# GpSimd's routing scatters move one step later, one behind each row sum and each normalisation

## The reference, cut to what matters

```python
x = x + _L0_attn_ref(_L0_cond_ref(x, cond_1024, ...), ...)
x = x + _L0_ffn_ref(_L0_cond2_ref(x, cond_1024, ...), ...)

# inside _L0_ffn_ref
attn = jax.nn.softmax(scores, axis=-1)
ao = jnp.einsum('bgqst,bgtd->bgqsd', attn, vb)
h1 = hidden_states + proj
x = ln2.reshape(-1, H)                                   # ln2: layer norm of h1
logits = x @ router_weight
top_p, top_i = jax.lax.top_k(jax.nn.softmax(logits, axis=-1), K)
...
padded_tokens = jnp.zeros((T, H), x.dtype).at[dst].set(x[order // K], mode='drop')
fc1 = jax.nn.gelu(jnp.einsum('ech,ehf->ecf', xt, moe_w1))
fc2 = jnp.einsum('ecf,efh->ech', fc1, moe_w2).reshape(T, H)
moe_out = jnp.zeros((N, H), hidden_states.dtype).at[padded_tid].add(weighted)
return h1 + moe_out.reshape(S, B, H)
```

## Time and profile before

| | us |
|---|---|
| median of 3 runs | 1206.87 (1204.98 to 1224.17) |
| the profiled execution | 1220.39 |
| its span, first to last instruction | 1218.6 |

### The profile page before, as it was taken

How to read it: one execution, slowest core, us unless ns; L and a number is a source line. 1 busy time by engine, 2 the same in 40 slices (tenths; PEclk the granted TensorE clock), 3 DMA queues, 4 the chain that set the end, 5 groups by cost and what they waited for, 6 DMA issues and landing times. The chain is left out here.

```text
span 1218.6 us, 25497 instructions
## 1 busy us (share of the span) xinstructions
PE 1120.3 (92%) x8218; PEld 1022.2 (84%) x8249; DVE 921.7 (76%) x2282; ACT 834.2 (68%) x1927; POOL 585.9 (48%) x564
## 2 busy tenths in 40 slices
PE   7899999999998899999987974989999999999994
PEld 4699999999997688788776863788999999999984
DVE  5677777776775689888888863897778888888872
ACT  2467666667665698888886872666676778778771
POOL 0012122121212244888887776377656546556545
PEclk9899999999998899999998996899999999999997
DMA  9524344353321032444444454378878778887853
GB/s 311 127 91 140 100 142 130 108 164 108 114 71 54 22 100 79 128 137 133 132 132 133 129 178 161 112 184 199 191 178 187 194 185 210 209 195 194 206 140 53
DMA packets 119056, 175.47 MB, mean 144 GB/s; under 512 B 13776, under 2 KB 88944, under 8 KB 118896
## 3 DMA queue, kind: packets, MB, share of 16 engines
q1 hardware_dynamic: 92336, 139.63, 37.7%
q0 software_dynamic: 26592, 34.24, 15.1%
HBM read 107.96 MB, written 67.69 MB: 144 GB/s over the span
## 5 line engine op out<-in xcount | busy, mean ns | idle before, releaser
L1268 POOL DMA_INDIRECT out_rows<-y,row x142 | 238.9, 1683 | 196.6 <-DVE y L1869 75.9
L178 PE MATMUL gh<-w2h,hh 128*128 128x256 f32 x568 | 160.8, 283 | 1.1 <-DVE y L1869 1.1
L180 PE MATMUL gh<-w2h,hl 128*128 128x256 f32 x568 | 160.7, 283 | 0.0
L179 PE MATMUL gh<-w2l,hh 128*128 128x256 f32 x568 | 160.7, 283 | 0.0
L1800 DVE TENSOR_TENSOR hl<-h,hh 128x512 fp32r<-128x512 f32 (+1 forms) x172 | 100.9, 596 | 67.1 <-ACT h L1483 62.1
L1246 POOL DMA_INDIRECT slot_rows<-kept,slot x112 | 117.9, 1053 | 32.8 <-issue 29.5
L1482 ACT ACTIVATE hh<-gw 128x512 fp32r<-128x512 f32 (+1 forms) x86 | 45.7, 531 | 107.6 <-issue 98.0
L178 PEld LDWEIGHTS gh<-w2h,hh 128*128 128x128 f32 x568 | 108.9, 192 | 2.2 <-issue 1.2
L179 PEld LDWEIGHTS gh<-w2l,hh 128*128 128x128 f32 x568 | 108.9, 192 | 1.0
L180 PEld LDWEIGHTS gh<-w2h,hl 128*128 128x128 f32 x568 | 108.9, 192 | 0.0
L819 POOL TENSOR_SCALAR spread<-mv 128x2 f32<-128x2 f32 x32 | 7.1, 221 | 211.6 <-DVE mv L967 211.2
(11 more groups left out here) (322 smaller groups left out, 3955.2 us busy)
## 6 DMA issues: line engine op xcount, KB each, us to landing
w1e<-in_moe_w SPq DMA_DIRECT2D x43, 512.0 KB
w2e<-in_moe_w SPq DMA_DIRECT2D x43, 512.0 KB
x_rows<-x SPq DMA_DIRECT2D x64, 256.0 KB, 2.4
xg<-x_rows SPq DMA_DIRECT2D x64, 256.0 KB
xr<-slot_rows SPq DMA_DIRECT2D x28, 532.0 KB
xT<-in_xT SPq DMA_DIRECT2D x32, 256.0 KB, 2.7
x<-in_x SPq DMA_DIRECT2D x32, 256.0 KB, 3.8
out_rows<-res SPq DMA_DIRECT2D x64, 128.0 KB
```

Source lines behind the costliest of these rows:

```text
L178: nc.tensor.matmul(out, at_a(ah), at_b(bh), start=first, stop=False, skip_group_check=True)
L179: nc.tensor.matmul(out, at_a(ah), at_b(bl), start=False, stop=False, skip_group_check=True)
L180: return nc.tensor.matmul(out, at_a(al), at_b(bh), start=False, stop=last, skip_group_check=True)
L1268: g.indirect_dma_start(out=out, out_offset=bass.IndirectOffsetOnAxis(ap=row[m % NR][:, t:t + 1], axis=0), in_=y[m % 2][:, t, :], in_offset ...
```

## The change

The four scatters of a step are taken out of its end. A generator hands them out one at a time: one after each row sum and one after each normalisation, and they are those of the step before (`scatters(k - 1 if k < I2 else k)`). Step 9 has none, the steps 10 to 31 carry those of the steps 9 to 30; step 31 also issues its own four at its end, and from step 32 on all is as it was. The wait for the blanking of the table moves ahead of step 0's normalisations. Nothing else changes, no operation is added or removed.

```diff
--- before.py
+++ after.py
@@ -1219,26 +1219,8 @@
             g.memset(half[:], -0.5).then_inc(halved, 1)
             pool.wait_ge(halved, 1)
 
-            def step(k, has):
-                if has(k - 2):
-                    after(pool, dve_did["mv"], k - 2, U2 - 1)
-                    g.tensor_scalar(spread[:], mv[:, :, 1], LN_EPS, None, ALU.add).then_inc(pool_did["spread"], 2)
-                    after(pool, pool_did["spread"], k - 2, U2 - 1)
-                    after(pool, act_did["nrm"], k - 3, U2 - 1)
-                    g.tensor_tensor(rstd[:], spread[:], half[:], ALU.pow).then_inc(pool_did["rstd"], 2)
-                    for u in places:
-                        after(pool, dve_did["h1"], k - 2, u)
-                        if k > 2:
-                            pool.wait_ge(stored[u], 16 * (k - 2))
-                        g.tensor_tensor(res[u][:], x12[u][:, 0, :], h1[u][:], ALU.add
-                                        ).then_inc(pool_did["res"], 1)
-                if has(k):
-                    for u in places:
-                        after(pool, dve_did["rden"], k, u)
-                        g.tensor_tensor(pw[k % 2][u][:], pw[k % 2][u][:], den[:, u, :].unsqueeze(2)
-                                        .broadcast_to([P, TG * NKV, S]), ALU.mult).then_inc(pool_did["soft"], 1)
-                if k == 0:
-                    pool.wait_ge(pr.blanked, 16 * (E + 1))
+            def scatters(k):
+
                 for m, pair, j in scattered_at(k):
                     pool.wait_ge(routed, m + 1)
                     after(pool, act_did["nrm"], pair, U2 - 1)
@@ -1247,6 +1229,37 @@
                             out=pr.slots, out_offset=bass.IndirectOffsetOnAxis(ap=pr.slot[:, c, j:j + 1], axis=0),
                             in_=pr.rows[:, j, :], in_offset=None, bounds_check=E * N - 1, oob_is_err=False,
                         ).then_inc(pr.scattered[0 if m <= EARLY_BATCH else 2 if m < LATE_BATCH else 1], 16)
+                        yield
+
+            def step(k, has):
+                if k == 0:
+                    pool.wait_ge(pr.blanked, 16 * (E + 1))
+                scatter = scatters(k - 1 if k < I2 else k)
+                if has(k - 2):
+                    after(pool, dve_did["mv"], k - 2, U2 - 1)
+                    g.tensor_scalar(spread[:], mv[:, :, 1], LN_EPS, None, ALU.add).then_inc(pool_did["spread"], 2)
+                    after(pool, pool_did["spread"], k - 2, U2 - 1)
+                    after(pool, act_did["nrm"], k - 3, U2 - 1)
+                    g.tensor_tensor(rstd[:], spread[:], half[:], ALU.pow).then_inc(pool_did["rstd"], 2)
+                    for u in places:
+                        after(pool, dve_did["h1"], k - 2, u)
+                        if k > 2:
+                            pool.wait_ge(stored[u], 16 * (k - 2))
+                        g.tensor_tensor(res[u][:], x12[u][:, 0, :], h1[u][:], ALU.add
+                                        ).then_inc(pool_did["res"], 1)
+                        if has(k):
+                            next(scatter, None)
+                if has(k):
+                    for u in places:
+                        after(pool, dve_did["rden"], k, u)
+                        g.tensor_tensor(pw[k % 2][u][:], pw[k % 2][u][:], den[:, u, :].unsqueeze(2)
+                                        .broadcast_to([P, TG * NKV, S]), ALU.mult).then_inc(pool_did["soft"], 1)
+                        next(scatter, None)
+                for _ in scatter:
+                    pass
+                if k == I2 - 1:
+                    for _ in scatters(k):
+                        pass
 
             pipeline(pool, step)
             out = d["out"].rearrange("t s n -> (t s) n")
```

More of the change, by code:

```diff
@@ L1220, in _ @@
             pool.wait_ge(halved, 1)
+            def scatters(k):
+                for m, pair, j in scattered_at(k):
+                    pool.wait_ge(routed, m + 1)
+                    after(pool, act_did["nrm"], pair, U2 - 1)
+                    for c in range(K):
+                        g.indirect_dma_start(
+                            out=pr.slots, out_offset=bass.IndirectOffsetOnAxis(ap=pr.slot[:, c, j:j + 1], axis=0),
+                            in_=pr.rows[:, j, :], in_offset=None, bounds_check=E * N - 1, oob_is_err=False,
+                        ).then_inc(pr.scattered[0 if m <= EARLY_BATCH else 2 if m < LATE_BATCH else 1], 16)
+                        yield
             def step(k, has):
+                if k == 0:
+                    pool.wait_ge(pr.blanked, 16 * (E + 1))
+                scatter = scatters(k - 1 if k < I2 else k)
                 if has(k - 2):
@@ L1239, in step @@
                                         .broadcast_to([P, TG * NKV, S]), ALU.mult).then_inc(pool_did["soft"], 1)
-                if k == 0:
-                    pool.wait_ge(pr.blanked, 16 * (E + 1))
-                for m, pair, j in scattered_at(k):
-                    pool.wait_ge(routed, m + 1)
-                    after(pool, act_did["nrm"], pair, U2 - 1)
-                    for c in range(K):
-                        g.indirect_dma_start(
-                            out=pr.slots, out_offset=bass.IndirectOffsetOnAxis(ap=pr.slot[:, c, j:j + 1], axis=0),
-                            in_=pr.rows[:, j, :], in_offset=None, bounds_check=E * N - 1, oob_is_err=False,
-                        ).then_inc(pr.scattered[0 if m <= EARLY_BATCH else 2 if m < LATE_BATCH else 1], 16)
+                        next(scatter, None)
[4 more added lines that the diff above has]
+                        pass
             pipeline(pool, step)
```

## The result

The kernel after takes 1252.99 us (median of 6 runs, 1248.91 to 1254.90), the kernel before, run beside it, 1208.82 (6 runs). The ratio is **1.0352, interval 1.0316 to 1.0389**: slower, by some 43 us (44 between the medians). The forecast of 1225 had the sign and less than half of the size, and the range to 1238 did not hold it.

The account below looks back on a forecast made before the run. GpSimd was taken to bound the kernel before, and the ring through the second normalisation the kernel after. The terms -1.0 + 8.9 + 8.4 - 2.7 + 5.1 gave +18.7 us, so 1225 us, range 1205 to 1238.

Parts of the forecast that it names:

- GpSimd bounds the kernel before; the change costs places, not work: Steps 11 to 25: GpSimd sets the pace at 9.98 us a step; nothing is removed or added, so places are costed.
- The row sums' ring: Row sum, SyncE's load, then `mv`: needs 9.6 us a step after the change and does not bind below that.
- Steps 9 to 11, -1.0: Step 9 loses its scatters, step 10 runs at GpSimd's pace: 18.9 us against 19.9.
- The ring through the second normalisation: Second normalisation, TensorE's queue, VectorE's maximum to `mv`: 21.2 us per two steps, +8.9 us over steps 11 to 25.
- The rule weighed: VectorE's two-port mode could lock out GpSimd and lengthen moved scatters; at its worst the sum would be the third rival's.
- Steps 25 to 29 at no cost: These steps are held by VectorE's table and TensorE's late scores, which the ring of 21.2 us hardly exceeds.
- Step 29's stall, 17.9 us: SyncE's load waits for scatters spread over step 29; step 30 starts 17.9 us after it, before 9.57: +8.4 us.
- Step 31, 14.7 us: Step 31 has eight scatters, so step 32 starts 14.7 us after it, against 9.64: +5.1 us.
- Step 30 to 31, -2.7: TensorE and ScalarE catch up during step 29's stall, so 12.35 us become GpSimd's 9.6.
- GpSimd stays the bound: Rival, chance 0.17: TensorE's order may have slack, so steps take 9.63 us; total 1212 us.
- faster: Rival, chance 0.08: scatter issue hides behind compute, at best a pace of 9.24 us a step; total 1198 us.
- Heavier: Rival, chance 0.22: scatters run at 1.44 us where they now stand; +27 us, total 1234 us.

Follow-up runs that it names:

- e11: The kernel before, with GpSimd's first instruction of a step (spread, variances plus a constant) given to VectorE; ratio 1.0047 to the kernel before.
- e4: The kernel after, with three scatters still ahead of the second normalisation but none between the row sums; ratio 1.0372 to the kernel before.
- e1: The kernel after, with all four scatters at the end of the step, behind both normalisations; ratio 1.0119 to the kernel before.
- e13: The kernel after, with two and four useless matmuls ahead of TensorE's two waits for the normalisations in steps 10 to 31; ratio 1.0331 to before.
- e14: The kernel after, with two and four useless matmuls ahead of TensorE's waits and each normalisation in two instructions of half the rows; ratio 1.0225 to before.
- e12: The kernel after, with all scatters at the step's end, SyncE's wait for early scatters behind its step, and no pile on step 31; ratio 1.0035 to before.
- e7: The kernel after, with each of GpSimd's normalisations in four instructions of a quarter each; ratio 1.0295 to the kernel before.
- e8: The kernel after, with four and eight useless matmuls ahead of TensorE's two waits for the normalisations in steps 10 to 31; ratio 1.0365 to before.

## Why the prediction was wrong

- **GpSimd bounds the kernel before; the change costs places, not work.** Right as to the work: its busy time stayed (121.8 us), the scatters' mean too (1047 ns), gaps 0.17. As a bound it was not alone: relieving it gave nothing (e11).
- **The row sums' ring does not bind.** Right (e4). **Steps 9 to 11, -1.0**: wrong, +0.9. Step 9's normalisation still ends 4.44 into it; in step 10, where scatters stand ahead of the normalisations, two VectorE instructions are held (500.28, 1.63 us, and 502.56, 2.06 us for a spreading of keys that takes 0.68 elsewhere), and GpSimd waits 2.17 us for `mv`.
- **The ring through the second normalisation sets the pace.** Right as a mechanism: idle time before `spread`, TensorE's wait for it, and the count of scatters ahead (e1 to e4) show it. A GpSimd step that waits alternates with one that doesn't, which changes nothing in the sum of a pair. It was this term that was mis-sized: 21.2 us for two steps, measured 22.5 to 24.1; +24.3 instead of +8.9.
- **The step that failed** is the sentence that took 5.42 us (transposes to maximum) and 7.37 (maximum to `mv`) from stretches of the kernel before and kept them. They are durations at full clock, and in before no small routing instruction that met a normalisation between the steps 10 and 30 took over 0.75 us. In the kernel after, the granted clock falls behind the ring's own wait on TensorE in five of seven rings, and the normalisations, moved later, hold VectorE's routing in all seven. The two legs together, 12.85 in the forecast with the 0.06 to the transposes, measure 13.8 us in the two rings where the clock stays and 14.5 to 15.4 in the five where it falls. The runs give, over steps 11 to 25: without the low clock 6.4 us less (e13); with shorter normalisations on top 4.0 less (e14, net of what halves cost GpSimd); 4.9 remain between its 153.6 and the forecast's 148.7. Most of that is the second normalisation, which ends near 8.9 in e14 where 8.4 was forecast, and the 0.17 us from `mv` to `spread`, a term that the forecast left out, seven times each. The order in which two causes are taken away decides how the shares fall, and one profile of the same code can differ by 4 us (e1, e12), so these are sizes, not decimals.
- **The rule weighed.** The forecast weighed VectorE's two-port mode, for what lengthens a scatter. What bore on this kernel was two inputs in SBUF, and the trace of before already held a case: the product with S at 476 ns beside S at 210, the same shape.
- **Steps 25 to 29 at no cost.** Wrong, +5.4. The sentence weighed the table and the late scores against a ring of 21.2 per two steps. At 23.8 (9.81 + 13.97 for steps 27 and 28, before 20.8) it is no longer "hardly exceeding".
- **Step 29's stall, 17.9 us.** Right, term by term: the last scatter ends 9.70 us into the step (forecast 9.63), SyncE gets on 2.6 later (2.5, a choice between 0 and 2.9, and here luck has a part, since later scatters landed up to 5.6 us after their issue), its second load is 0.87 behind (0.86), 3.65 to VectorE's second add (3.66), 1.30 to `mv` (1.3), and 0.17 that the forecast left out: 18.29. **Step 31, 14.7 us.** Right: 14.59. **Step 30 to 31, -2.7**: measured -1.6; the step has 1.28 us of waiting for `mv`, where 9.6 us without a wait were forecast. That the tail reaches the end nearly whole is what e1 and e12 suggest, about 10 us for the 12 net in the steps, within the wide bounds given above.
- **The rivals.** "GpSimd stays the bound" and "faster" fell with the first scatter ahead. "Heavier" had the nearest time, 1234, for a reason that is not there. None took in that the things beside the ring get slower too, which is why the range ended at 1238.
- **Better than both kernels?** None of the orders tried beats before. e11 and e12, the nearest, are at 1.0047 and 1.0035.

## What to carry to other kernels

When a move makes a ring bind, its legs are not the durations they had with slack: price them once more with the waits that the ring itself creates. Ask what clock the matmuls behind the new wait get, and which VectorE instructions with two SBUF inputs the moved GpSimd work now meets. That an engine is never idle doesn't say that relieving it pays: 0.38 us a step taken off it bought nothing here.

## What the runs showed of the hardware

- A VectorE instruction with both inputs in SBUF that starts beside a GpSimd product of SBUF operands, or up to 0.6 us ahead of its recorded start, ends 0.10 us after it: 0.20 us became 1.64 and 1.73 in the rows shown. With the product in quarters the mean is back at 0.23 (e7). The other way round, a pair of half products that takes 1.20 us took 1.52 where such an instruction of VectorE had started 0.28 us ahead (e14).
- A wait of 2.10 us on TensorE was followed by granted clocks of 0.78 and 0.55 in one ring, and 16 weight loads took 3.06 us; behind the same wait in another ring they took 1.72. Two and four useless matmuls inside the waits kept the clock at 0.99 in that stretch (e13); with twice as many TensorE was busy throughout and the stretch took 168.4 us instead of 164.1 (e8).
- An indirect scatter of 128 rows issued by GpSimd holds it for 0.97 to 1.5 us in nearly every case, wherever it stands, and at most for 1.9; the gap ahead of it is 0.17 us behind a compute instruction and 0.30 behind another scatter. Where the profile of after has a landing (16 of them), it came 2.6 to 5.6 us after the issue.
